# The sums of a probability tile move ahead of its values, and get a semaphore of their own

## The chip, the cores and the metric

One core of a Trainium2 chip runs the whole kernel. The metric is the device time of one execution in microseconds (us). The kernel before takes 2410.32 us, the median of 3 runs (2405.26 to 2411.59).

## The reference, cut to what matters

A transformer block with adaptive layer norm, on x of shape (2, 2048, 512), 16 heads of 32, a hidden layer of 1024, all in f32:

```
h   = ln(x) * (1 + scale_msa) + shift_msa
q, k, v = h @ Wq + bq, h @ Wk + bk, h @ Wv + bv         # (2, 2048, 16, 32) each
A   = softmax(q k^T / sqrt(32))                          # over the 2048 keys
x   = x + gate_msa * ((A v) @ Wo + bo)
out = x + gate_mlp * (gelu(ln(x)*(1+scale_mlp)+shift_mlp @ W1 + b1) @ W2 + b2)
```

Two batches of 16 heads make 32 heads of attention with 2048 queries and 2048 keys each. The softmax needs three things of a head: a maximum of each query's scores, the exponentials, and the sum of each query's exponentials. The change is in how that sum and the product A v are ordered.

## The kernel before, in words

The kernel has three stages: projections of the 8 chunks of 512 rows (0 to about 362 us in the profile), the 32 heads (362 to about 1948 us), then the output projection and the MLP of the 8 chunks (to 2407.8 us). All order is written out by hand, one instruction stream for each engine, with semaphores between them.

**A head is 16 steps**, one for each tile t of 128 keys. In step t TensorE (`head`, L1426) does, in this order:

- The scores of tile t, transposed (128 keys by 512 queries), for four groups r = 0 to 3 of 512 queries. Each r uses one group of 32 rows of the array and one PSUM bank, and is made of four products: L1387, L1389, L1391, and L1396, which subtracts the query's maximum.
- Between them, four products of the next head (`max_tile`, L1375), of which only the maximum is wanted. They go in the order r = 2, 3 (near the start of the step) and r = 0, 1 (near its end). VectorE reduces each of them (L1106) and so frees its bank.
- `values` (L1411): the product of tile t-1's exponentials with v, four groups of 32 columns side by side, accumulated over the head in bank 7 (`O_BANK`).
- `take_sums` (L1400): in some steps, the sums. There are two kinds. For the tiles of `pe_tiles` (2, 5, 8, 11 and 15; for the last head 2, 5, 8 and 11 to 15) TensorE multiplies the exponentials of the tile by ones. The others are added up by GpSimd (L742) into `psum_acc`, and TensorE multiplies this total by ones, in step 4 of the next head (`ACC_STEP`). So heads have sums in steps 0, 3, 4, 6, 9 and 12.

ScalarE makes four exponentials in each step (L893), from the score banks into one of four slots of `prob` in SBUF. After those of step t it takes the sums of step t: it waits for them, copies the bank to SBUF (L871), waits for its own copy, and issues a DMA that stores it (L873). In step 0 of a head it first copies the finished output of the head before (L859).

**Banks.** Eight PSUM banks: number 7 holds the output, the other seven are handed out by `bank_table`, a small planner that runs when the kernel is built. It walks through the steps, and gives each use (S: a score, M: a product for the maximum, D: sums) the bank that by its estimate is free first. Its estimates within a step of 11.7 units are in

```
    until = {"S": (8, 10, 12, 14), "M": (11, 13, 6, 8), "D": 16}
```

and the uses of one step are entered in the order S0, S1, M2, M3, S2, S3, M0, M1, then D. These are up to nine uses for seven banks, so a bank is used again within its own step. Before a use, `bank_free` makes TensorE wait for whoever reads the bank's last contents: `exp_ok` for an S (ScalarE's exponential), `a_max` for an M (VectorE's reduction), `sums_ok` for a D. Followed through the table, the sums of the heads 0 to 30 get these banks: in steps 0, 3, 6 and 12 the bank of the same step's score r = 0 (122 uses); in steps 4 and 9 the bank of the same step's M for r = 3, which is the step's second reduction on VectorE (60 uses). Two more uses, in the first two heads, are one of each kind: 123 S in all, 61 M. The last head has no M and fixed banks: its sums all use bank 2, one after the other.

**Semaphores.** `pv_mm` counts the tiles whose exponentials TensorE has finished with. In the kernel before it is raised by the values of a tile without sums of its own, and by the sums, which come after the values, of a tile with them. ScalarE waits for it before it overwrites a slot of `prob` four tiles later, before its copy of the output, and before its copy of a tile's sums. SyncE waits for it once in a head.

Of the kernel before, what the change touches and what calls it, by code (L numbers as in the profile page):

```python
# [33 lines left out]
CH = 512  # L34
# [4 lines left out]
NT = L // P  # L39
NQ = L // CH  # L40
MIX = D // DH

RING = 4
# [4 lines left out]
FILLS = NQ * NT  # L48
# [5 lines left out]
START = 1  # L54
# [9 lines left out]
def pool_tiles(g):  # L64

    return [0, 1, 3, 4, 6, 7, 9, 10] + ([12, 13, 14] if g < G - 1 else [])


def pe_tiles(g):

    return [t for t in range(NT) if t not in pool_tiles(g)]
# [7 lines left out]
def adds_before(g, k=0):  # L79

    return HALVES * (g * (len(pool_tiles(0)) - 1) + k)
# [55 lines left out]
USES, USES_END = bank_table()  # L137
# [5 lines left out]
def block_kernel(nc, x, cT, wq, wk, wv, wo, w1, w2, wada, bqT, bkT, b1T, badaT, bada, bv, bo, b2, out):  # L143
# [8 lines left out]
    with ExitStack() as ctx:  # L152
# [3 lines left out]
        def sem(name):  # L156
            return ctx.enter_context(nc.semaphore(name))
# [8 lines left out]
        def view(t, at, *shape):  # L166
            n = 1
            for s in shape:
                n *= s
            ap = t[:, at:at + n]  # L170
            names = "abcd"[:len(shape)]
            if len(shape) == 1:
                return ap
            return ap.rearrange(f"p ({' '.join(names)}) -> p {' '.join(names)}",
                                **{k: s for k, s in zip(names[1:], shape[1:])})
# [28 lines left out]
        sums = [view(work, at, CH) for at in (3072, 1024)]  # L204
        o_st = [view(work, at, CH) for at in (2048, 2560)]
        w2_st = o_st[1]
        prob = view(work, 5632, RING, L)
# [99 lines left out]
        b_mm = sem("b_mm")  # L307
        exp_ok = sem("exp_ok")
        pv_mm = sem("pv_mm")
        add_ok = sem("add_ok")  # L310
        den_mm = sem("den_mm")
        gate_out = sem("gate_out")
# [44 lines left out]
        def sums_buffer(n):  # L357
            return (n - 1) % 2 if n < SUMS_END else 0

        def sums_before(n, b):  # L360

            return sum(sums_buffer(m) == b for m in range(1, n))
# [418 lines left out]
        def _(act):  # L781
# [79 lines left out]
            def take_sums(uses):  # L861

                for g, d, bank, _, n in uses:
                    b = sums_buffer(n)
                    if d < len(pe_tiles(g)):
                        act.wait_ge(pv_mm, START + g * NT + pe_tiles(g)[d] + 1)
                    else:
                        act.wait_ge(den_mm, START + g + 1)
                    if sums_before(n, b):
                        act.wait_ge(sums_out[b], 16 * sums_before(n, b))  # L870
                    nc.scalar.activation(sums[b], ps[:, bank, :], ACT.Copy).then_inc(sums_ok, 1)  # L871
                    act.wait_ge(sums_ok, n)
                    act.dma_start(sums_dram[g * ND + d:g * ND + d + 1, :].rearrange("o (r q) -> (o r) q", q=CH),  # L873
                                  sums[b][0:P:DH, :]).then_inc(sums_out[b], 16)
# [363 lines left out]
        def _(pe):  # L1238
# [118 lines left out]
            def bank_free(use):  # L1357

                bank, before, _ = use
                if before:  # L1360
                    kind, n = before
                    if kind == "S":
                        pe.wait_ge(exp_ok, START + n)
                    elif kind == "M":
                        pe.wait_ge(a_max, n)
                    else:
                        pe.wait_ge(sums_ok, n)

            def max_tile(g, q, r, use):


                bank_free(use)
                u = g % HI_BUF
                at = slice(r * DH, (r + 1) * DH)
                nc.tensor.matmul(ps[:, use[0], :], q_hi[u][at, q // NQ * P:(q // NQ + 1) * P],  # L1375
                                 k_hi[u][at, q % NQ * CH:(q % NQ + 1) * CH], start=True, stop=True).then_inc(a_mm, 1)

            def score_part(g, t, r, part):

                u, w = g % HI_BUF, g % TWO  # L1380
                use = USES[g][t]["scores"][r]
                at = slice(r * DH, (r + 1) * DH)
                keys = slice(t * P, (t + 1) * P)
                o = ps[:, use[0], :]
                if part == 0:
                    bank_free(use)
                    nc.tensor.matmul(o, k_hi[u][at, keys], q_hi[u][at, :], start=True, stop=False)  # L1387
                elif part == 1:
                    nc.tensor.matmul(o, k_lo[w][at, keys], q_hi[u][at, :], start=False, stop=False)  # L1389
                elif part == 2:  # L1390
                    nc.tensor.matmul(o, k_hi[u][at, keys], q_lo[w][at, :], start=False, stop=False)  # L1391
                else:
                    if t == 0:
                        pe.wait_ge(maxT_in, (g + 1) * (16 * MAX_PIECES))
                    row = slice(r * DH, r * DH + 1)
                    nc.tensor.matmul(o, minus_r[row, :], m_row[w][row, :], start=False, stop=True).then_inc(b_mm, 1)  # L1396

            def sums_of(src, bank):
                for j in range(NQ):
                    mm = nc.tensor.matmul(ps[j * DH:(j + 1) * DH, bank, :], ones[:, 0:DH], src(j), start=True, stop=True)  # L1400
                return mm

            def values(g, t):

                pe.wait_ge(exp_ok, START + g * FILLS + (t + 1) * NQ)
                if t == 0 and g:
                    pe.wait_ge(o_raw, g)
                elif t == 0:
                    pe.wait_ge(a_max, FIRST_FILLS)
                for j in range(NQ):  # L1410
                    mm = nc.tensor.matmul(ps[j * DH:(j + 1) * DH, O_BANK, :], v_sb[g % TWO][:, t, :], prob[:, t % RING, j * CH:(j + 1) * CH],  # L1411
                                          start=(t == 0), stop=(t == NT - 1))
                if t not in pe_tiles(g):
                    mm.then_inc(pv_mm, 1)

            def take_sums(uses):

                for g, d, *use in uses:
                    bank_free(use)
                    if d < len(pe_tiles(g)):  # L1420
                        sums_of(lambda j: prob[:, pe_tiles(g)[d] % RING, j * CH:(j + 1) * CH], use[0]).then_inc(pv_mm, 1)
                    else:
                        pe.wait_ge(add_ok, START + adds_before(g, len(pool_tiles(g)) - 1))
                        sums_of(lambda j: psum_acc[g % 2][:, j * CH:(j + 1) * CH], use[0]).then_inc(den_mm, 1)

            def head(g, between={}):  # L1426

                per_head = FILLS // NQ
                q = g * per_head + (LEAD if g else FIRST_QUADS)

                pe.wait_ge(lo_in[g % TWO], 16 * (g // TWO * LOADS_LO + (LOADS_LO if g % TWO else 1)))
                for t, uses in enumerate(USES[g]):
                    scores, tops = uses["scores"], uses["max"]
                    if tops[0] and q % per_head == 0:
                        ahead = 1 + q // per_head

                        pe.wait_ge(hi_in[ahead % HI_BUF], (ahead // HI_BUF + (ahead % HI_BUF == 2)) * (16 * LOADS_HI))
                    for part in range(5):
                        if part < 4:
                            score_part(g, t, 0, part)  # L1440
                            score_part(g, t, 1, part)
                        if part:
                            if part == 4 and tops[0]:
                                for r in (0, 1):
                                    max_tile(1 + q // per_head, q % per_head, r, tops[r])
                            score_part(g, t, 2, part - 1)
                            score_part(g, t, 3, part - 1)
                        elif tops[0]:
                            for r in (2, 3):
                                max_tile(1 + q // per_head, q % per_head, r, tops[r])  # L1450
                    if tops[0]:
                        q += 1
                    if t:
                        values(g, t - 1)
                    elif g:
                        values(g - 1, NT - 1)
                    take_sums(uses["sums"])
                    if t in between:
                        between[t]()

# [4 lines left out]
            for g in range(G - 1):  # L1465
                head(g)
# [28 lines left out]
            between = {STEP_PROJECT + t: lambda t=t: first_projection(t) for t in range(TT)}  # L1495
            between[STEP_TRANSPOSE] = lambda: transposes3(0, (0, 1))
            head(G - 1, between)
            values(G - 1, NT - 1)
            take_sums(USES_END[:1])
            transposes3(0, (2, 3))  # L1500
            take_sums(USES_END[1:])

            def mlp1(n, f):
# [71 lines left out]
```

## Time and profile before

| | us |
|---|---|
| median of 3 runs | 2410.32 (2405.26 to 2411.59) |
| the profiled execution | 2409.57 |
| its span, first to last instruction | 2407.8 |
| TensorE busy | 2355.9 (98%) |
| VectorE, GpSimd, ScalarE busy | 1743.4, 1672.5, 1403.7 |
| heads, 362.2 to 1883.4 (31 of 32) | 1521.20 |
| granted clock of TensorE in the heads | 1.00 of full |

Busy times of TensorE are modelled by the profiler: matmuls overlap each other, and a wait can sit inside a stretch that counts as busy. So the starts of the instructions are read here, more than their shares. "PE" rows are matmuls, "PEld" rows the loads of their weights, which come ahead of each matmul and carry its waits.

### The profile page before, as it was taken

How to read it: one execution, taken by the hardware profiler on the slowest of the kernel's cores; microseconds unless marked ns; L12 is line 12 of the kernel's file. 1: busy time of each engine (PE TensorE's matmuls, PEld its weight loads, DVE VectorE, ACT ScalarE, POOL GpSimd, SP SyncE). 2: the span in 40 equal slices, each digit the busy share in tenths (PEclk: the TensorE clock that was granted, in tenths of full speed). 3: DMA queues.
4: the chain of work that ended last, by engine and by line, in shares of the span. 5: the costliest groups of instructions: out<-in, count | busy, mean ns of one | idle time of the engine just before them, and what ended most of it. 6: DMA issues, size and time to landing. Idle time of an engine off the chain costs nothing.

```text
span 2407.8 us, 48495 instructions
## 1 busy us (share of the span) xinstructions
PE 2355.9 (98%) x19312; PEld 1340.1 (56%) x19312; DVE 1743.4 (72%) x2866; ACT 1403.7 (58%) x2591; POOL 1672.5 (69%) x806
## 2 busy tenths in 40 slices
PE   6999989999999999999999999999999989999998
PEld 4788864444444444444444444444444458888887
DVE  4445747888888888888888888888888656656653
ACT  3232317777777777777777777777777642222221
POOL 0001029999999999999999999999999842233320
PEclk9999999999999999999999999999999989999999
DMA  8566452333323232322323232322323222222210
GB/s 278 186 206 202 134 169 70 75 73 69 82 62 86 61 86 60 79 60 60 78 62 77 57 81 56 83 56 65 74 63 72 68 85 80 70 70 70 71 36 35
DMA packets 208653, 211.14 MB, mean 88 GB/s; under 512 B 116253, under 2 KB 149021, under 8 KB 198889
## 3 DMA queue, kind: packets, MB, share of 16 engines
q1 hardware_dynamic: 204898, 200.91, 32.0%
q0 software_dynamic: 1248, 5.51, 0.9%
q8 instruction: 152, 2.49, 0.5%
q10 hardware_dynamic: 2280, 1.63, 0.3%
q14 instruction: 75, 0.61, 0.1%
HBM read 147.11 MB, written 60.59 MB: 86 GB/s over the span
## 4 chain that ended last, share of the span: by engine, by line
PE 93%; ACT 2%; DMA 2%; DVE 1%; issue 1%; SPq 0%; POOL 0%; ACTq 0%; POOLq 0%
PE ps L1411 21%; PE ps L1268 20%; PE ps L1387 11%; PE ps L1375 11%; PE ps L1518 7%; PE ps L1400 7%; PE ps L1389 6%; PE ps L1391 5%; PE ps L1396 3%; DMA q_lo<-work 1%; PE ps L1277 1%; ACT work L871 1%; PE ps L1308 1%; DVE acts_r L1146 0%; DVE stats L990 0%
## 5 line engine op out<-in xcount | busy, mean ns | idle before, releaser
L1106 DVE TENSOR_REDUCE part_max<-ps 128x1 f32<-128x512 f32 x1968 | 1222.2, 682 | 265.1 <-PE ps L1375 265.1
L893 ACT ACTIVATE work<-ps 128x512 f32<-128x512 f32 x2048 | 1057.8, 603 | 322.7 <-PE ps L1396 280.3
L742 POOL TENSOR_TENSOR work<-work 128x1024 f32<-128x1024 f32 x314 | 740.6, 2413 | 34.8 <-ACT work L893 34.3
L742 POOL TENSOR_TENSOR gate<-gate,work 128x1024 f32<-128x1024 f32 x288 | 675.1, 2401 | 14.9 <-ACT work L893 14.9
L1411 PE MATMUL ps<-work 128*32 128x512 f32 x4096 | 546.6, 606 | 0.1
L1375 PE MATMUL ps<-acts_r 32*128 32x512 f32 x1328 | 412.4, 471 | 3.3 <-ACT work L893 1.8
L1268 PE MATMUL ps<-acts_r,weights_r 128*128 128x512 f32 x1536 | 381.7, 399 | 4.6 <-DVE acts_r L1018 3.9
L1268 PEld LDWEIGHTS ps<-acts_r,weights_r 128*128 128x128 f32 x1536 | 292.0, 192 | 69.9 <-issue 4.7
L1387 PEld LDWEIGHTS ps<-acts_r 32*128 32x128 f32 x1408 | 141.6, 182 | 305.2 <-DVE part_max L1106 175.2
L1387 PE MATMUL ps<-acts_r 32*128 32x512 f32 x1408 | 291.5, 466 | 1.4 <-issue 0.8
L1389 PE MATMUL ps<-acts_r 32*128 32x512 f32 x1408 | 252.6, 393 | 0.0
L1375 PEld LDWEIGHTS ps<-acts_r 32*128 32x128 f32 x1328 | 179.8, 183 | 110.1 <-DVE part_max L1106 89.2
L946 ACT ACTIVATE work<-ps,b_sb 128x512 f32<-128x512 f32 x64 | 44.1, 690 | 332.8 <-PE ps L1268 332.8
L692 POOL TENSOR_TENSOR var_eps<-var_eps,mv 128x4 f32<-128x4 f32 x16 | 3.2, 202 | 329.6 <-DVE mv L996 329.6
L1396 PE MATMUL ps<-acts_r,minus_r 1*128 1x512 f32 x1024 | 228.7, 442 | 0.0
L1396 PE MATMUL ps<-m_odd,minus_r 1*128 1x512 f32 x1024 | 225.3, 438 | 0.0
L766 POOL TENSOR_TENSOR work<-work,gate_b 128x512 f32<-128x512 f32 x60 | 86.5, 1472 | 169.2 <-DMA work<-in_x 148.8
L1375 PE MATMUL ps<-acts_r,w_r 32*128 32x512 f32 x640 | 198.8, 470 | 0.8
L1268 PE MATMUL ps<-weights_r,acts_r 128*128 128x512 f32 x768 | 188.9, 399 | 6.4 <-DVE acts_r L1146 6.4
L1400 PE MATMUL ps<-work,ones 128*32 128x512 f32 x1432 | 187.3, 595 | 0.0
L1391 PE MATMUL ps<-w_r,acts_r 32*128 32x512 f32 x1024 | 184.9, 395 | 0.0
L1518 PE MATMUL ps<-w_r,acts_r 128*128 128x512 f32 x768 | 184.4, 391 | 0.0
(104 smaller groups left out, 2816.1 us busy)
## 6 DMA issues: line engine op xcount, KB each, us to landing
acts_r<-k_lo SPq DMA_DIRECT2D x124, 256.0 KB, 4.6
acts_r<-k_hi SPq DMA_DIRECT2D x120, 256.0 KB, 4.6
work<-in_x SPq DMA_DIRECT2D x16, 1024.0 KB, 6.2
q_hi<-work SPq DMA_DIRECT2D x32, 256.0 KB, 2.7
q_lo<-work SPq DMA_DIRECT2D x32, 256.0 KB, 3.3
k_hi<-work SPq DMA_DIRECT2D x32, 256.0 KB, 2.5
k_lo<-work SPq DMA_DIRECT2D x32, 256.0 KB, 3.2
v_rows<-work SPq DMA_DIRECT2D x32, 256.0 KB, 2.0
```

The lines of the kernel that those rows point to most:

```text
L742: nc.gpsimd.tensor_tensor(acc[:, at], first, prob[:, t % RING, at], ALU.add).then_inc(add_ok, 1)
L893: nc.scalar.activation(prob[:, t % RING, j * CH:(j + 1) * CH], ps[:, bank, :], ACT.Exp, scale=SCALE).then_inc(exp_ok, 1)
L1106: nc.vector.tensor_reduce(part_max[:, r * TT + q // NQ, q % NQ:q % NQ + 1], ps[:, bank, :], AX.X, ALU.max).then_inc(a_max, 1)
L1268: mm = nc.tensor.matmul(o, lhs(s, kk), rhs(r, kk), start=(kk == 0 and s == r), stop=(kk == KC - 1 and s == 1))
L1375: nc.tensor.matmul(ps[:, use[0], :], q_hi[u][at, q // NQ * P:(q // NQ + 1) * P], k_hi[u][at, q % NQ * CH:(q % NQ + 1) * CH], start=True, s ...
L1387: nc.tensor.matmul(o, k_hi[u][at, keys], q_hi[u][at, :], start=True, stop=False)
L1389: nc.tensor.matmul(o, k_lo[w][at, keys], q_hi[u][at, :], start=False, stop=False)
L1391: nc.tensor.matmul(o, k_hi[u][at, keys], q_lo[w][at, :], start=False, stop=False)
L1396: nc.tensor.matmul(o, minus_r[row, :], m_row[w][row, :], start=False, stop=True).then_inc(b_mm, 1)
L1400: mm = nc.tensor.matmul(ps[j * DH:(j + 1) * DH, bank, :], ones[:, 0:DH], src(j), start=True, stop=True)
L1411: mm = nc.tensor.matmul(ps[j * DH:(j + 1) * DH, O_BANK, :], v_sb[g % TWO][:, t, :], prob[:, t % RING, j * CH:(j + 1) * CH], start=(t == 0) ...
L1518: mm = nc.tensor.matmul(ps[:, 4 + t, :], g_r[:, f % 4, s, t * P:(t + 1) * P], w2_r[:, r, f, :], start=(f == 0 and s == r), stop=(f == FB - ...
```

## The change

The sums of a step are issued before its values instead of after them, in `head` and at the end of the last head. Every tile's values now raise `pv_mm`. The sums of a tile raise a new semaphore, `tile_sums`, and ScalarE waits for that before it copies them. As the sums now come first, they get the wait for the exponentials of the tile that only the values had. The bank table is the same, and so is ScalarE's own order.

```diff
+        tile_sums = sem("tile_sums")
...
                     if d < len(pe_tiles(g)):
-                        act.wait_ge(pv_mm, START + g * NT + pe_tiles(g)[d] + 1)
+                        act.wait_ge(tile_sums, g * len(pe_tiles(0)) + d + 1)
                     else:
                         act.wait_ge(den_mm, START + g + 1)
...
-                if t not in pe_tiles(g):
-                    mm.then_inc(pv_mm, 1)
+                mm.then_inc(pv_mm, 1)
...
                     bank_free(use)
                     if d < len(pe_tiles(g)):
-                        sums_of(lambda j: prob[:, pe_tiles(g)[d] % RING, j * CH:(j + 1) * CH], use[0]).then_inc(pv_mm, 1)
+                        pe.wait_ge(exp_ok, START + g * FILLS + (pe_tiles(g)[d] + 1) * NQ)
+                        sums_of(lambda j: prob[:, pe_tiles(g)[d] % RING, j * CH:(j + 1) * CH], use[0]).then_inc(tile_sums, 1)
...
                     if tops[0]:
                         q += 1
+
+                    take_sums(uses["sums"])
                     if t:
                         values(g, t - 1)
                     elif g:
                         values(g - 1, NT - 1)
-                    take_sums(uses["sums"])
...
             head(G - 1, between)
+            take_sums(USES_END[:1])
             values(G - 1, NT - 1)
-            take_sums(USES_END[:1])
             transposes3(0, (2, 3))
             take_sums(USES_END[1:])
```

## Rows read from the trace of the kernel before

**Rows 1.** The heads: busy time (and instructions) of each engine in the stretch.

```profile
core 0: us, PE busy (x) PEld busy (x) DVE busy (x) ACT busy (x) POOL busy (x), PEclk, DMA share, GB/s
362.20:1883.40 1521.20, 1518.44 (x15349) 684.89 (x15348) 1248.81 (x2089) 1155.93 (x2211) 1467.64 (x632) 1.00 0.31 70
```

**Rows 2.** Waits of TensorE's weight loads over the span: total us, times, longest.

```profile
PEld ps L1375 <- DVE part_max L1106: 132.7, 425, 0.5
...
PEld ps L1400 <- issue: 61.0, 204, 0.3
PEld ps L1400 <- ACT work L893: 37.2, 124, 0.4
PEld ps L1400 <- DVE part_max L1106: 18.3, 61, 0.3
```

**Rows 3.** Timeline, TensorE, head 15: values (L1411) of steps 5 to 9, one step's sums.

```profile
start us, us, engine line op out<-in xcount [idle before <-releaser]
1112.56 1.06 PE L1411 MATMUL ps<-work 128*32 128x512 f32 x8
...
1115.27 1.07 PE L1411 MATMUL ps<-work 128*32 128x512 f32 x8
...
1116.16 1.04 PE L1400 MATMUL ps<-work,ones 128*32 128x512 f32 x8
...
1118.86 1.06 PE L1411 MATMUL ps<-work 128*32 128x512 f32 x8
...
1121.58 1.07 PE L1411 MATMUL ps<-work 128*32 128x512 f32 x8
...
1124.44 0.64 PE L1411 MATMUL ps<-work 128*32 128x512 f32 x4
```

**Rows 4.** Timeline, weight loads around the values of step 6.

```profile
1115.27 0.16 PEld L1411 LDWEIGHTS ps<-work 128*32 128x32 f32 x8 [0.24 <-issue]
1115.73 0.13 PEld L1400 LDWEIGHTS ps<-work,ones 128*32 128x32 f32 x4 [0.30 <-ACT work L893]
```

**Rows 5.** Timeline: first exponential of steps 6 and 12, and the values of step 12.

```profile
1114.88 0.60 ACT L893 ACTIVATE work<-ps 128x512 f32<-128x512 f32 x1 [0.61 <-PE ps L1396]
...
1133.03 0.60 ACT L893 ACTIVATE work<-ps 128x512 f32<-128x512 f32 x1 [0.60 <-PE ps L1396]
...
1133.46 0.64 PE L1411 MATMUL ps<-work 128*32 128x512 f32 x4
```

**Rows 6.** Timeline, step 4: first two reductions; the last M's load; the values.

```profile
1107.80 0.69 DVE L1106 TENSOR_REDUCE part_max<-ps 128x1 f32<-128x512 f32 x1 [1.09 <-PE ps L1375]
...
1108.41 0.68 DVE L1106 TENSOR_REDUCE part_max<-ps 128x1 f32<-128x512 f32 x1
...
1108.55 0.18 PEld L1375 LDWEIGHTS ps<-acts_r 32*128 32x128 f32 x1 [0.30 <-DVE part_max L1106]
...
1108.97 1.06 PE L1411 MATMUL ps<-work 128*32 128x512 f32 x8
```

**Rows 7.** Timeline, steps 8 and 9: load of the last M of each; VectorE in step 9.

```profile
1121.14 0.18 PEld L1375 LDWEIGHTS ps<-acts_r 32*128 32x128 f32 x1 [0.27 <-DVE part_max L1106]
...
1123.15 0.25 DVE L1118 RECIPROCAL rec_c<-den_c 128x16 f32<-128x16 f32 x1
...
1123.32 0.63 DVE L1106 TENSOR_REDUCE part_max<-ps 128x1 f32<-128x512 f32 x1
...
1123.87 0.67 DVE L1106 TENSOR_REDUCE part_max<-ps 128x1 f32<-128x512 f32 x1
...
1124.01 0.18 PEld L1375 LDWEIGHTS ps<-acts_r 32*128 32x128 f32 x1 [0.44 <-DVE part_max L1106]
```

**Rows 8.** Timeline, steps 0 to 2: ScalarE's copies and store, its second exponential, TensorE.

```profile
1098.11 0.60 ACT L859 ACTIVATE work<-ps 128x512 f32<-128x512 f32 x1 [0.35 <-PE ps L1400]
1098.61 0.59 ACT L871 ACTIVATE work<-ps 128x512 f32<-128x512 f32 x1
1099.23 0.48 ACTq L873 DMA_DIRECT2D partial_sums<-work  x1
...
1099.70 1.06 PE L1411 MATMUL ps<-work 128*32 128x512 f32 x8
...
1100.33 0.59 ACT L893 ACTIVATE work<-ps 128x512 f32<-128x512 f32 x1
...
1100.97 0.18 PEld L1375 LDWEIGHTS ps<-acts_r 32*128 32x128 f32 x2
...
1102.68 0.64 PE L1411 MATMUL ps<-work 128*32 128x512 f32 x4
```

**Rows 9.** Timeline, ScalarE, steps 3 and 4: exponentials, copy of sums, its store.

```profile
1105.01 2.07 ACT L893 ACTIVATE work<-ps 128x512 f32<-128x512 f32 x4 [0.61 <-PE ps L1396]
1107.39 0.60 ACT L871 ACTIVATE work<-ps 128x512 f32<-128x512 f32 x1 [0.32 <-PE ps L1400]
1108.02 0.48 ACTq L873 DMA_DIRECT2D partial_sums<-work  x1
1108.63 0.60 ACT L893 ACTIVATE work<-ps 128x512 f32<-128x512 f32 x1 [0.64 <-POOL work L742]
```

**Rows 10.** All copies of sums (L871) and what ended ScalarE's idle time before them.

```profile
L871 ACT ACTIVATE work<-ps 128x512 f32<-128x512 f32 x195 | 116.7, 598 | 59.9 <-PE ps L1400 59.1 <-DMA partial_sums<-work 0.7
```

**Rows 11.** Timeline, end of the last head: last sums, then ScalarE's way into the MLP.

```profile
1947.39 1.04 PE L1400 MATMUL ps<-work,ones 128*32 128x512 f32 x8
...
1948.49 0.60 ACT L871 ACTIVATE work<-ps 128x512 f32<-128x512 f32 x1 [2.28 <-PE ps L1400]
1949.12 0.48 ACTq L873 DMA_DIRECT2D partial_sums<-work  x1
1949.79 0.78 ACT L806 ACTIVATE acts_r<-ps,mod 128x512 fp32r<-128x512 f32 x1 [0.69 <-ACT work L871]
```

## The prediction, made before the result was known

> **What bounds the kernel now.** I read the busy times by stretch first. The heads hold 1521 of the 2408 us, and there TensorE is busy 1518 us at the full granted clock, with VectorE at 82%, GpSimd at 96% and ScalarE at 76% [rows 1]. So only what TensorE does or waits for can move the time. Then the timeline, by the starts of the values in one head. A step without sums takes 2.71 or 2.72 us (1112.56 to 1115.27, 1118.86 to 1121.58), one with sums 3.59 (1115.27 to 1118.86): the sums cost 0.87 us of TensorE, and they do so in either order [rows 3].
>
> Inside such a step TensorE does wait, although it counts as busy. The list of waits shows the last product for a maximum (L1375) held by VectorE's reduction [rows 2]. Step 4 shows how: the first reduction ends at 1107.80 + 0.69 = 1108.49, the load of the product that needs its bank starts at 1108.55, and the values come 0.42 us later, at 1108.97 [rows 6]. Step 9 shows that such a wait has no slack. There VectorE first does a reciprocal, its first reduction ends at 1123.32 + 0.63 = 1123.95 and the load starts at 1124.01. That is 2.43 us after the values before it (1121.58), where step 8 has 1121.14 - 1118.86 = 2.28; and the step takes 1124.44 - 1121.58 = 2.86 us where step 8 takes 2.72 [rows 3, 7]. 0.15 later in the wait, 0.14 later in the step: what delays TensorE's stream here goes into the time at full price.
>
> **The change part by part.** First, the bank of the sums. They use a bank that was read in the same step. Before, they stand behind 0.89 us of values (1115.27 to 1116.16, [rows 3]), and their first weights are loaded 0.46 us into them, at 1115.73 [rows 4]. After, they are to start where the values start now. I call that moment V and ask when each bank is free.
> - Banks of a score (123 sums). The reader is the first exponential of the same step. In step 12 it ends at 1133.03 + 0.60 = 1133.63, and V is 1133.46: 0.17 after V. In step 6 it is 1114.88 + 0.60 = 1115.48 against 1115.27: 0.21 after V [rows 5].
> - Banks of a product for a maximum (61 sums). The reader is the second reduction. In step 4: 1108.41 + 0.68 = 1109.09 against 1108.97, 0.12 after V [rows 6].
> - From the end of a reader to TensorE's load, the trace has 0.06 us after VectorE (1108.49 to 1108.55, [rows 6]) and 0.05 after ScalarE (1100.33 + 0.59 = 1100.92 to 1100.97, [rows 8]).
>
> So all 184 sums of the heads 0 to 30 have to wait behind V, where now the values cover it. Following each through the bank table and the trace, with 0.053 us for the hand-over, the medians are 0.21 us in steps 3, 6 and 12, 0.24 in step 0, and 0.16 in steps 4 and 9. The sums over all: 93 waits of steps 3, 6, 9 and 12 make 20.4 us, 30 of step 0 make 7.4, and 61 behind reductions 9.8. Together **37.5 us**, or 1.21 a head. The list of waits has the same 184 or so: loads of L1400 held 124 times by ScalarE and 61 by VectorE [rows 2]. Nothing gives it back. The values behind the sums need only TensorE itself, the next step starts that much later, and its own waits (the reduction at its start) run from its own start.
>
> Here a rule of the chip speaks on the size. In the trace the wait sits on the load of the weights: L1400's load is what stands idle until ScalarE has ended, and the values' matmuls run on meanwhile [rows 4]. The Trainium skill, page "TensorE: Matmul & The Clock Gate", section "Step-by-step: what each phase is for", says that TensorE may pull weight loads ahead of running matmuls, while matmuls stay in program order. The second half says that the values can't overtake the sums that wait, which is the loss above. The first half would make it smaller if the sums' loads went in while the bank is still in use; how much is worked out under the rivals.
>
> Second, the new wait for the exponentials, 156 times in these heads. Those of step 4 are used in step 5, at 1112.56, and ScalarE ended them at about 1110.7 (four of 0.52 us from 1108.63, as the four from 1105.01 take 2.07, [rows 9]). So it is satisfied 1.9 us early. It stands in the queue ahead of a load that waits anyway. No row shows the instruction by itself. It can cost from nothing to a hand-over of 0.05 us each, 8 us in all; I take nothing, by the nearest row, the load of the values, which carries that same wait now and starts without a gap it would explain [rows 4].
>
> Third, ScalarE. It copies the sums earlier. Now it is idle 59.1 us in all before 195 copies [rows 10], 0.32 in step 4: its exponentials are done at 1105.01 + 2.07 = 1107.08 and the copy starts at 1107.39 [rows 9]. With the sums 0.89 - 0.21 = 0.68 us earlier against the end of the values, that idle time goes, and no more than that: its own exponentials stand before the copy. The store (L873) follows, 0.3 earlier too. Who gains? TensorE waits for ScalarE visibly in step 2, which takes 1102.68 - 1099.70 = 2.98 us where others take 2.72: a product for a maximum waits for the second exponential of step 1 (ends 1100.92, load 1100.97), which is late behind two copies and a store (1098.11, 1098.61, 1099.23) [rows 8]. But that row of work starts with the copy of the head's output, which needs the values of tile 15. These now come last, and end when the sums end now. So nothing is gained there, and 31 times 0.26 = 8 us is the bound for all of ScalarE's gain in the heads. I take 0.
>
> Fourth, `pv_mm`. For tiles with sums it is raised at the same point as before, the end of both products. For tile 3 it comes 0.87 us later, as step 4 holds the sums of the total; ScalarE needs that slot three steps on. The other tiles don't change. Cost 0; with its cover gone it would be 31 times 0.87.
>
> Fifth, the end. In the last head the sums use bank 2 alone, whose last reader was a step before, so no wait is added. At its end ScalarE waits for the last sums until 1948.49, copies, stores, and at 1949.79 starts the work from which the MLP begins [rows 11]. The sums come 0.88 us earlier there (1947.39 is where they start now, after the values), so this chain starts up to 0.9 earlier. Behind it is a DMA chain that starts elsewhere, so between 0 and -0.9; I take **-0.8**.
>
> The sum: the profiled execution, 2409.57, + 37.5 - 0.8 = 2446.3 us. Its own time is 0.75 below the median of the three runs, so against that median the forecast is 2410.3 + 36.7 = **2447.0 us**, 1.5% slower.
>
> **The rivals.**
> - *Only VectorE's banks count.* The profile infers releasers, and ScalarE raises `exp_ok` four times a step, so the 124 waits could be ticks of a later exponential while the right one was long past. Then 9.8 - 0.8: 2419 us. Against it: the table gives the score r = 0 of the same step, and that exponential does end after V [rows 5]. 0.05.
> - *Loads go ahead of the wait.* Each wait would be shorter by the load of 0.11 us (a load of L1400 spans 0.13 for four, [rows 4]): 184 times (0.204 - 0.11) = 17 us, less 0.8: 2427 us. This is what the rule of the Trainium skill quoted above would give. Against it: both loads that were seen held start only after the release, 0.05 or 0.06 later [rows 6, 8]. 0.08.
> - *The whole gap shows.* The list of waits has 37.2 + 18.3 = 55.5 us before these loads [rows 2], 0.30 each. If restarting behind a wait costs that, or the added waits on TensorE cost theirs, it is 2410.3 + 55.5 - 0.8 = 2465 us. Against it: part of the 0.30 is the load's ordinary place behind the values, as 204 loads have it with no releaser. 0.10.
> - *ScalarE frees TensorE: faster.* If the banks are free at V after all (no wait added) and ScalarE's earlier copy removes the late exponential of step 1, the 8 us of step 2 come back: 2410.3 - 8 - 0.8 = 2401.5 us. It decides as soon as ScalarE's gain in a head is above the 1.21 us of the waits. Against it: ScalarE can gain only the 0.26 of step 2 in a head, and the order of its copies there stays. 0.03.
> - *No net change*: the copies move, nobody waits for them, and the bank waits stay covered by something I don't see. 2410 us. 0.04.
>
> **How the numbers follow.** My forecast has 0.70, with 2439 to 2455 as its own range: the hand-over of 0.05, and readers that end 0.04 earlier or later. The range for 8 in 10 goes down to the loads that go ahead and part of the way up to the whole gap: 2425 to 2458. About 0.3%, 7 us, is what a measurement of this kernel can tell from no change. Faster by more than that 0.03, within it 0.05, slower 0.92 (my forecast and the first three rivals have 0.93; a little of it lies near the bound).
>
> **What would show it.** In the trace after: a step with sums takes 3.79 us instead of 3.59 in steps 3, 6 and 12, and 3.75 in steps 4 and 9, a head 50.3 instead of 49.1; steps without sums keep their 2.72, and step 2 its 2.98. The loads of the sums start 0.05 us after the first exponential or the second reduction has ended, and the values 0.88 after them. ScalarE's idle time before its copies is nearly gone. I am wrong if the sums start right behind the scores (then the banks were free), if the sum steps grow by 0.3 or more, or if steps without sums become shorter, which would be ScalarE's gain.

## The result: 1.6% slower, and the profile after

The changed kernel takes 2448.2 us (median of 6 runs, 2444.15 to 2449.46), against 2410.3 us before (6 runs). The ratio is 1.0157, with a 95% interval of 1.0147 to 1.0168. The forecast was 2447.0: 36.7 us more, where the interval has 35.4 to 40.5. The profiled execution took 2446.26 us, its span is 2444.5.

The heads first, in the same stretch as in [rows 1], from the values of head 0's first tile to those of head 31's first tile:

```profile
core 0: us, PE busy (x) PEld busy (x) DVE busy (x) ACT busy (x) POOL busy (x), PEclk, DMA share, GB/s
361.47:1919.82 1558.35, 1531.38 (x15349) 685.87 (x15348) 1249.98 (x2089) 1139.21 (x2211) 1466.22 (x632) 1.00 0.30 68
```

1558.35 against 1521.20: 37.2 us more, which is the whole difference of the two spans (36.7), within half a us. The instructions are the same in number, the clock is 1.00 in both. TensorE's busy time grew by 13 us only. The rest stands as idle time, 27 us where it was 3.

Where it went can be read step by step. For the table the starts of the last product of each step's scores were taken from both traces. A step is the time from one to the next (this includes the values, the sums and the next scores); the numbers are medians over heads 1 to 29, in us. The prediction counted by the starts of the values instead, so its step 2 (2.98 us) is column 1 here, and its step 9 (2.86 us) is column 8:

```
step     0      1      2      3      4      5      6      7      8      9      10     11     12     13 to 15
before   3.580  3.004  2.707  3.579  3.581  2.721  3.580  2.722  2.858  3.580  2.722  2.722  3.581  2.72
after    3.813  2.996  2.711  3.794  3.747  2.726  3.793  2.725  2.858  3.740  2.723  2.719  3.792  2.72
```

The six steps with sums are longer, by 0.23 (step 0), 0.21 (3, 6, 12), 0.17 (4) and 0.16 (9). All others are as they were. A head takes 50.32 instead of 49.10.

Step 6 of head 15 in the timeline shows one such wait, to be laid beside [rows 3 to 5]. First TensorE's matmuls and loads, then ScalarE's four exponentials of the step before and the first of this one:

```profile
start us, us, engine line op out<-in xcount [idle before <-releaser]
1129.85 1.07 PE L1412 MATMUL ps<-work 128*32 128x512 f32 x8
...
1132.78 1.06 PE L1401 MATMUL ps<-work,ones 128*32 128x512 f32 x8
1133.67 1.04 PE L1412 MATMUL ps<-work 128*32 128x512 f32 x8
...
1136.37 1.07 PE L1412 MATMUL ps<-work 128*32 128x512 f32 x8
```

```profile
1132.14 0.18 PEld L1376 LDWEIGHTS ps<-acts_r 32*128 32x128 f32 x1 [0.30 <-DVE part_max L1107]
1132.14 0.18 PEld L1397 LDWEIGHTS ps<-m_odd,minus_r 1*128 1x128 f32 x2
1132.78 0.16 PEld L1401 LDWEIGHTS ps<-work,ones 128*32 128x32 f32 x8 [0.45 <-ACT work L894]
1133.24 0.13 PEld L1412 LDWEIGHTS ps<-work 128*32 128x32 f32 x4 [0.30 <-ACT work L894]
```

```profile
1129.43 2.07 ACT L894 ACTIVATE work<-ps 128x512 f32<-128x512 f32 x4 [1.19 <-PE ps L1397]
1132.13 0.60 ACT L894 ACTIVATE work<-ps 128x512 f32<-128x512 f32 x1 [0.64 <-PE ps L1397]
```

The exponential that reads the bank ends at 1132.73, and the sums' load starts at 1132.78. It comes 0.64 us after the load of the last M (1132.14). In the kernel before, the values came 0.42 us after that load [rows 6]. So the wait is 0.22. The exponentials that the values need had ended at 1129.43 + 2.07 = 1131.50. The values follow the sums by 0.89 (1133.67 - 1132.78), the price that the two paid each other before.

Step 4, with a bank that VectorE reads, beside [rows 6]: the second reduction ends at 1125.53 + 0.68 = 1126.21, the load starts at 1126.27. Followed through the bank table, all 184 loads of the heads 0 to 30 are like these two: each starts 0.050 to 0.054 us after the end of the instruction that read its bank. In the trace of before 182 of them start 0.2 us or more after it.

```profile
1124.93 0.69 DVE L1107 TENSOR_REDUCE part_max<-ps 128x1 f32<-128x512 f32 x1 [1.30 <-PE ps L1376]
...
1125.53 0.68 DVE L1107 TENSOR_REDUCE part_max<-ps 128x1 f32<-128x512 f32 x1
...
1126.27 0.16 PEld L1401 LDWEIGHTS ps<-gate,ones 128*32 128x32 f32 x8 [0.41 <-DVE part_max L1107]
```

The list of waits has the two groups of [rows 2] that name a reader. The idle time before the sums' loads grew from 37.2 to 57.4 us and from 18.3 to 24.8, with the same number of waits but one. That is 26.7 us, less than the loss, because the ordinary idle time is another: 0.30 us before a load that comes second, as the sums did, and 0.24 before one that comes first ([rows 4], the values' load). By an estimate from these, 82.2 - 184 × 0.24 = 38 us of it is waiting.

```profile
PEld ps L1401 <- ACT work L894: 57.4, 123, 0.8
PEld ps L1412 <- ACT work L894: 49.1, 161, 0.7
PEld ps L1401 <- DVE part_max L1107: 24.8, 61, 0.4
```

The middle row is a warning. It names ScalarE as the releaser of the values' loads 161 times. Yet in 159 of the 161 the exponentials that the load needs ended over 1.1 us before (1131.50 against 1133.24 above); only two, in the last steps of head 30, start 0.05 us behind one. It is the newest tick of the semaphore that the profile finds, while the load stands in its ordinary place behind the sums. A releaser's name alone is no proof: the end of the named instruction must lie right before the start that it released, and be one that is waited for.

And ScalarE, beside [rows 9, 10]: the idle time before its copies of the sums that it spent on TensorE went from 59.1 us to 0.6. It was not a gain. The exponentials wait for TensorE instead, 418.4 us where it was 280.3.

```profile
L872 ACT ACTIVATE work<-ps 128x512 f32<-128x512 f32 x195 | 121.9, 625 | 5.9 <-DMA partial_sums<-work 5.3 <-PE ps L1401 0.6
...
L894 ACT ACTIVATE work<-ps 128x512 f32<-128x512 f32 x2048 | 1057.9, 604 | 423.4 <-PE ps L1397 418.4
```

### The profile page after: what moved, and what is told of

It reads as the page before. It is cut to its first block, busy times and chain, and to the rows that moved or that the text cites. A ratio compares the mean times of both kernels' runs of the same rounds, so it can differ in the third digit from the quotient of the medians.

```text
span 2444.5 us, 48658 instructions
## 1 busy us (share of the span) xinstructions
PE 2368.1 (97%) x19312; PEld 1340.5 (55%) x19312; DVE 1737.7 (71%) x2866; ACT 1386.6 (57%) x2591; POOL 1669.4 (68%) x806
## 4 chain that ended last, share of the span: by engine, by line
PE 83%; DVE 7%; ACT 5%; issue 3%; DMA 2%; ACTq 0%; SPq 0%; POOL 0%; POOLq 0%
PE ps L1269 20%; PE ps L1412 18%; PE ps L1388 10%; PE ps L1401 8%; PE ps L1520 7%; PE ps L1376 6%; DVE part_max L1107 5%; PE ps L1390 5%; ACT work L894 3%; PE ps L1392 3%; PE ps L1397 2%; PE ps L1278 1%; ACT work L872 1%; DMA q_lo<-work 1%; PE ps L1309 1%
## 5 line engine op out<-in xcount | busy, mean ns | idle before, releaser
L894 ACT ACTIVATE work<-ps 128x512 f32<-128x512 f32 x2048 | 1057.9, 604 | 423.4 <-PE ps L1397 418.4
L1388 PEld LDWEIGHTS ps<-acts_r 32*128 32x128 f32 x1408 | 148.7, 183 | 306.5 <-DVE part_max L1107 173.4
L1376 PEld LDWEIGHTS ps<-acts_r 32*128 32x128 f32 x1328 | 180.5, 183 | 110.7 <-DVE part_max L1107 90.0
L1401 PE MATMUL ps<-work,ones 128*32 128x512 f32 x1432 | 192.5, 610 | 23.0 <-ACT work L894 7.8
L1412 PEld LDWEIGHTS ps<-work 128*32 128x32 f32 x4096 | 101.1, 109 | 196.1 <-issue 147.0
```

The lines of the kernel that those rows point to most:

```text
L894: nc.scalar.activation(prob[:, t % RING, j * CH:(j + 1) * CH], ps[:, bank, :], ACT.Exp, scale=SCALE).then_inc(exp_ok, 1)
```

## The experiments

Four kernels ran together with the kernel before on one chip (before: 2409.43 us, 20 runs), then four more on another occasion (before: 2408.53, 11 runs). All were profiled, and timed 4 to 11 times each. "The theory" in the expectations is that of the prediction: each sum waits for the reader of its bank, at full price.

### The semaphores alone

```diff
-                    take_sums(uses["sums"])
+                    ahead = g == G - 1 or sums_ahead(t, uses["sums"])    # sums_ahead: always False here
+                    if ahead:
+                        take_sums(uses["sums"])
                     if t:
                         values(g, t - 1)
                     elif g:
                         values(g - 1, NT - 1)
+                    if not ahead:
+                        take_sums(uses["sums"])
```

> The changed kernel with the old order (values, then sums) in the heads 0 to 30; the semaphores stay separate, and the last head stays as changed. Theory (each wait for a bank goes into the time): the 184 waits, 37.5 us, are covered again. Beside that the values of tile 15 now release ScalarE's copy of the output by themselves, 0.88 us before the sums are done, so its queue in steps 0 and 1 runs about 0.3 us earlier, and the late second exponential that stretches the step from 1 to 2 by 0.27 to 0.28 us is in time: 31 times 0.27 = 8 us. Expected: steps with sums 3.58, step 1 2.72 instead of 3.00, time 2402 us, 0.3% under the kernel before. Rival (only the order matters, the semaphore is idle weight): 2410 us. Rival (the separate semaphore itself costs, an added increment and wait): the steps with sums stay above 3.60 and the time lies above 2415 us.

Measured: 2399.43 us, ratio 0.9957 (0.9944 to 0.9969), faster than both kernels. All six steps with sums are back at 3.58, and the step after step 1's scores takes 2.727 instead of 3.00. So the added semaphore and its waits cost nothing that shows. The order alone was the loss. And the separate semaphore, without the order, is a gain, which the prediction had not seen. ScalarE's stretch from step 0 to step 1 of head 15, beside [rows 8]:

```profile
1091.65 2.06 ACT L894 ACTIVATE work<-ps 128x512 f32<-128x512 f32 x4 [0.68 <-PE ps L1400]
1093.58 0.63 ACT L860 ACTIVATE work<-ps 128x512 f32<-128x512 f32 x1
1094.07 0.63 ACT L872 ACTIVATE work<-ps 128x512 f32<-128x512 f32 x1
1094.73 0.48 ACTq L874 DMA_DIRECT2D partial_sums<-work  x1
1095.34 1.58 ACT L894 ACTIVATE work<-ps 128x512 f32<-128x512 f32 x3 [0.64 <-PE ps L1400]
```

```profile
1095.66 1.07 PE L1415 MATMUL ps<-work 128*32 128x512 f32 x8
```

The copy of the output (L860) starts right behind the exponentials, with no idle time, where before it had 0.35 us of it: it now waits for the values alone and no more for the sums behind them. The exponentials of step 1 start 0.32 us ahead of that step's values (1095.34 against 1095.66). In the kernel before, the first started at 1099.84, 0.14 behind the values. TensorE gets its bank in time, and a head takes 48.87 us instead of 49.10. That is 7.1 us over the heads 0 to 30 (1516.2 against 1523.3); the medians are 10 us apart, and the interval has 7.5 to 13.5. I can't place the rest: from one profile to another the time ahead of the first head's scores differs by up to 3 us (353.6 to 356.8), and so does the time after the last scores (462.3 to 465.2), whatever the kernel.

### The sums ahead in some steps only

All three runs are the kernel above with another `sums_ahead`:

```diff
-            return False
+            return bool(uses) and uses[0][3][0] == "M"             # only banks of a product for a maximum
+            return bool(t and uses) and uses[0][3][0] == "S"       # only banks of a score, not step 0
+            return t == 0                                          # only step 0
```

> As the kernel with the semaphores alone, but in the 61 steps of heads 0 to 30 whose sums take the bank of a product for a maximum (steps 4 and 9) the sums go ahead. Theory: only those wait, 0.16 us each, 9.8 us: steps 4 and 9 take 3.74, steps 0, 3, 6 and 12 3.58, time 2402 + 10 = 2412 us if the run with the semaphores alone has 2402, in any case 10 us above it. Rival (the order itself costs, whatever the bank, because the array changes between two kinds of products in another place): 61 of 184 of the whole 38 us, 12.6 us, or 0.21 a step in these steps as in all others.

Measured: 2409.59 us, 10.2 above the semaphores alone. Steps 4 and 9 take 3.746 and 3.740, steps 0, 3, 6 and 12 3.58. The 0.16 of these steps is the wait that the theory has for their reader; the rival, a cost of the order by itself whatever the bank, had 0.21 in each.

> As the kernel with the semaphores alone, but in the 93 steps 3, 6, 9 and 12 of heads 0 to 30 whose sums take the bank of a score the sums go ahead; step 0 keeps the old order. Theory: they wait 0.21 to 0.22 us each for the first exponential, 20.4 us: these steps take 3.79, steps 4, 9 and 0 3.58; time 20 us above the run with the semaphores alone, 2422 us. Rival (what the profile names as ScalarE's release is only a tick of the same semaphore, VectorE's banks alone count): no difference, 2402 us.

Measured: 2417.07 us, 17.6 above the semaphores alone. Steps 3, 6 and 12 take 3.791, 3.792 and 3.794, the others 3.58. The steps show the expected 0.21; over the heads 0 to 30 of the two profiles it is 19.1 us (1535.3 against 1516.2). VectorE's banks are not the only ones that count.

> As the kernel with the semaphores alone, but in step 0 of each head the sums of the head before go ahead. Theory: two costs in one place. The sums wait 0.24 us for the bank of the first score (30 times, 7.4 us), and the values of tile 15 come last again, so ScalarE's copy of the output and with it the second exponential of step 1 are late again (31 times 0.27, 8 us): step 0 3.81, step 1 3.00, time 15 us above the run with the semaphores alone, 2417 us. Rival (ScalarE's queue is not what stretches the step from 1 to 2): only 7 us above it, step 1 unchanged from that run.

Measured: 2415.62 us, 16.2 above the semaphores alone. Step 0 takes 3.812, and the step after it 3.003: both costs are there. ScalarE's queue is what stretches that step.

In medians of a head: 48.87 with the semaphores alone, then + 0.32 + 0.62 + 0.47 for the three parts, which makes 50.28; the changed kernel has 50.32. The parts account for the whole.

### ScalarE copies the sums first

```diff
-                    if g and t == 0:
-                        take_output(g - 1)
                     take_sums(USES[g][t]["sums"])
+                    if g and t == 0:
+                        take_output(g - 1)
```

> The changed kernel, with one edit on ScalarE: in step 0 it copies the sums before the output of the head before, not after it. Theory: with the sums ahead they are ready 0.88 us before the values, so ScalarE can use the time in which it would wait for the values, and the second exponential of step 1 is in time again. Step 1 goes from 3.00 to 2.73, 31 times 0.27 = 8 us: 2440 us. The waits for the banks stay: steps with sums 3.74 to 3.81. Rival (step 1 is long in the changed kernel for another reason, a wait of TensorE for the copy of the output): no change or worse, since that copy now comes later, 2448 us or more.

Measured: 2434.73 us, ratio to before 1.0109 (1.0096 to 1.0122), 5 below the expected 2440 and 13.5 below the changed kernel's median, which was taken on another occasion (before: 2410.3 there, 2408.53 here, so 1.8 us of it is the occasion). The step tables give the cleaner number: the step after step 1's scores went from 2.996 to 2.723, a head from 50.32 to 50.07, so 0.25 a head or 7.8 us. The steps with sums keep their waits (3.79 to 3.81 and 3.74). Of the rest, 2.4 us lie before the heads begin (353.7 against 356.1 us in the two profiles), where the kernels are alike; I can't tell it from the spread of runs. The order of ScalarE's two copies is worth what the theory says, and it can't pay for the waits.

### Shorter readers, and their control

In steps 3, 4, 6, 9 and 12 of heads 1 to 30 the reader of the sums' bank covers half of the columns.

```diff
-                        nc.scalar.activation(prob[:, t % RING, j * CH:(j + 1) * CH], ps[:, bank, :], ACT.Exp, ...
+                        w = CH // 2 if short(g, t, "S", bank) else CH
+                        nc.scalar.activation(prob[:, t % RING, j * CH:j * CH + w], ps[:, bank, 0:w], ACT.Exp, ...
...
-                    nc.vector.tensor_reduce(part_max[...], ps[:, bank, :], AX.X, ALU.max)
+                    w = CH // 2 if r == 3 and short(*at, "M", bank) else CH
+                    nc.vector.tensor_reduce(part_max[...], ps[:, bank, 0:w], AX.X, ALU.max)
```

> The changed kernel, with the readers of the banks that the sums take made shorter, in steps 3, 4, 6, 9 and 12 of heads 1 to 30: the exponential of that score, or the reduction of that product, covers 256 of its 512 columns (half of a tile's probabilities, and half of a block of the maximum, are left out). The order, the semaphores and every wait stay. Theory: the readers end 0.2 to 0.3 us earlier, near or before the moment at which the sums can start, and the waits of 0.21 and 0.16 us vanish: these steps go from 3.79 and 3.74 to about 3.58 to 3.62, step 0 keeps 3.81. 27 to 30 us less: 2418 to 2421 us. Rival (the cost is in the order of the products, not in the wait): 2447 us, or what the control below gains from the shorter work alone.

> Control for the run before: the kernel with the semaphores alone (values, then sums) with the same shorter exponentials and reductions. Theory: where the values cover the readers, it doesn't matter when these end: no difference from the run with the semaphores alone, 2399.4 us, steps with sums 3.58. Rival (the shorter work speeds the steps by itself): clearly under 2395 us.

Measured: 2416.71 us and 2398.83 us. With the sums ahead, the shorter readers take 31 us off, 29.4 in the heads 0 to 30 of the two profiles (1560.4 to 1531.0); the time is 1 us below the expected range, and the kernel before was 1.8 us lower on this occasion. With the values ahead, they take off nothing (2399.43 without them; 1516.2 and 1515.4 in the heads). The steps 3, 4, 6, 9 and 12 take 3.58 in both, step 0 keeps its 3.816 in the first. In the timeline the sums' load of step 6 has its ordinary distance of 0.43 us behind the load before it. The shortened exponential ends at 1117.36 + 0.38 = 1117.74, so its bank is free just in time, and a wait of 0.01 us at most is left:

```profile
1117.36 0.38 ACT L898 ACTIVATE work<-ps 128x256 f32<-128x256 f32 x1 [0.64 <-PE ps L1402]
```

```profile
1117.37 0.18 PEld L1402 LDWEIGHTS ps<-m_odd,minus_r 1*128 1x128 f32 x2
1117.80 0.16 PEld L1406 LDWEIGHTS ps<-work,ones 128*32 128x32 f32 x8 [0.25 <-ACT work L898]
```

This is the strongest of the runs. Order, semaphores, banks and waits are those of the changed kernel, and only the work of the readers, and with it the moment at which the banks are free, differs; the control shows that the shorter work by itself is worth nothing.

### The price of a wait, away from the sums

The semaphores alone, and VectorE's denominators after the reductions of step 9 instead of 8:

```diff
-                    if t == STEP_RECIP and g:
+                    if t == STEP_RECIP + 1 and g:
                         denominators(g - 1)
```

> The kernel with the semaphores alone, with VectorE's sum and reciprocal of the denominators issued after the reductions of step 9 instead of step 8. It tests the price of a wait away from the sums: in the trace of before they delay the first reduction of step 9 and stretch that step by 0.14 us. After step 9, which has sums, VectorE is idle over 1 us, which hides them. Theory (a wait inside a step goes into the time at full price): step 8 goes from 2.86 to 2.72, 30 times 0.14 = 4 us: 2395 us. Rival (such waits are made up for later in the head): 2399 us, the 0.14 turning up in another step.

Measured: 2394.99 us, ratio to before 0.9944 (0.9932 to 0.9956), the lowest median here. The semaphores alone had 0.9957 (0.9944 to 0.9969) on the other occasion; the intervals overlap, so the traces decide. Step 8 takes 2.721 instead of 2.859, no other step is longer by more than 0.01, a head is 48.70 instead of 48.87, and the heads 0 to 30 take 1511.0 instead of 1516.2 us. VectorE's row shows the cover:

```profile
1118.30 0.31 DVE L1117 TENSOR_REDUCE den_c<-sums_c 128x16 f32<-128x96 f32 x1
1118.65 0.25 DVE L1119 RECIPROCAL rec_c<-den_c 128x16 f32<-128x16 f32 x1
1119.48 1.89 DVE L1107 TENSOR_REDUCE part_max<-ps 128x1 f32<-128x512 f32 x3 [0.58 <-PE ps L1379]
```

The next reduction still waits 0.58 us for TensorE, with both small operations done.

## Why the prediction was right, and where it was off

- **The banks.** Predicted: 184 waits, 37.5 us, medians of 0.24 in step 0, 0.21 in 3, 6 and 12, and 0.16 in 4 and 9. Measured: 0.23, 0.21, 0.17 and 0.16, and 37.1 us over the heads 0 to 30 (1560.4 against 1523.3 between the same products). The split by the reader of the bank, and the run in which the readers end earlier, show the cause. Two readings behind it were wrong, and neither enters the sum. [rows 4] does not show the sums' load held by ScalarE: the exponential ended at 1115.48 [rows 5] and the load came at 1115.73, in its ordinary place; so the list of waits in [rows 2] was no second witness for the 184 waits, as it named readers that were not waited for. And the wait for the exponentials stands 154 times in these heads, not 156.
- **Full price, no return.** The steps without sums stayed as they were, as the prediction said from one case (step 9). Moving the denominators showed it in the other direction.
- **The hand-over and the loads.** Both 0.05 us. The load of the sums never ran ahead of its wait (0.050 to 0.054 us behind the reader, 184 times), so the rival with 2427 us is out: the part of the Trainium skill's rule ("TensorE: Matmul & The Clock Gate", "Step-by-step: what each phase is for") that would have made the loss smaller does nothing for a load that carries the wait itself. The other part, that matmuls stay in program order, is what the trace shows: the values stood ready and started 0.89 us after the sums.
- **The added wait for the exponentials.** Predicted 0, bounded by 8 us. Steps with sums grew by the bank's wait alone, so 0 is right within 0.01 a step.
- **ScalarE.** Predicted: it gets its copies done earlier and nobody gains. So it was. The reason given for step 1, that the values of tile 15 still end when the sums ended, was right too; what I did not draw from it is that the same semaphore with the old order would let them go earlier. I had the 8 us in hand as "the bound for all of ScalarE's gain" and did not ask which half of the change could earn them.
- **The end.** This step failed: predicted was that the MLP's first work comes 0.8 us earlier. It started 6.58 us after the last scores' last product, where it was 6.47, and no profile of a kernel with the sums ahead there has less than 6.57. (The whole time after the last scores, 464.8 against 464.5 us, can't show it, as it differs by up to 3 us between profiles.) The sums were indeed earlier, but ScalarE did not take them. In the last head all sums pass through one buffer, and its copy waited for the store before it to land:

```profile
1982.50 0.49 ACTq L874 DMA_DIRECT2D partial_sums<-work  x1
1984.92 0.60 ACT L872 ACTIVATE work<-ps 128x512 f32<-128x512 f32 x1 [2.45 <-DMA partial_sums<-work]
```

In [rows 11] the same copy starts 0.06 us after the sums' end (1947.39 + 1.04 = 1948.43), so I took TensorE for its only bound. The store ahead of it was issued at 1946.25 there:

```profile
1946.25 0.48 ACTq L873 DMA_DIRECT2D partial_sums<-work  x1
```

The trace has its landing at 1948.37, 0.06 us before the sums were done: two waits ended together, and the removal of one showed the other. So the term is nothing, and not -0.8. That the forecast (2447.0) lies only 1.2 us from the measured median is partly luck, with an interval 5 us wide; the steps of the heads are the better witness for the parts.

The rivals: the whole gap (2465) is out by the step lengths, VectorE's banks alone (2419) by the run on the banks of scores, loads ahead of the wait (2427) by the loads' starts, and "faster" and "no change" by the time. But the mechanism of the "faster" rival, the late exponential of step 1, was real. It belonged to the other half of the change.

## What to carry to other kernels

Before two pieces of work on the bottleneck engine change places, look up for each what it waits for, and when that is ready measured from the *earlier* place: here the values waited for nothing and covered 0.2 us that the sums needed, 184 times. A planner that reuses PSUM banks inside one step makes the order part of its plan; its table would have to be made again with the order. No run here did that, so whether the sums can go ahead at no cost with another table stays open. And a semaphore that stands for two things should be split where it is waited for, with the order left alone: that part by itself made this kernel 0.4% faster.

## What the runs showed beyond that

- Two copies by ScalarE back to back start 0.49 us apart although each takes 0.60 to 0.63 (1093.58 and 1094.07). So adding up their durations overstates its queue.
- The copies of the sums got longer where they follow the exponentials without a gap, 625 ns on average against 598 [rows 10]. The store behind such a copy is issued 0.66 us after the copy's start (1094.07 to 1094.73), where it was 0.62 (1098.61 to 1099.23, [rows 8]); in the steps of TensorE this doesn't show.
